# Attention with routed experts: VectorE copies the accumulator out unscaled, GpSimdE joins the halves and multiplies by reciprocal sums turned to 64 partitions

## What is computed

```python
q, k, v = x @ Wq + bq, x @ Wk + bk, x @ Wv + bv      # 8 heads ("d") of width h = 64
scores = jnp.einsum('bdsh,bdth->bdst', q, k) / np.sqrt(8)
weights = jax.nn.softmax(scores, axis=-1)
feats = jnp.einsum('bdst,bdth->bdsh', weights, v)    # S = 2048 rows, 2048 keys
x = layernorm(x + feats.reshape(B, S, F) @ Wo + bo)
# then, per row: top 6 of 64 experts by sigmoid(x @ w_gate), capacity 256 rows per expert,
# silu(g) * v of x @ w_up[e], times w_down[e], weighted sum; plus a shared expert
x = layernorm(x + shared + routed)
```

## Time and profile before

| | us |
|---|---|
| median of 3 runs | 1292.33 |
| lowest, highest | 1290.95, 1292.90 |
| span of the profiled execution | 1289.5 |
| TensorE busy in the span | 1255.7 (97%) |
| VectorE, ScalarE, GpSimdE busy | 998.2, 919.8, 513.2 |

### The profile page before, as it was taken

The page is one execution under the profiler, slowest core; times in us unless marked ns, Lnnn a source line. Parts: engine busy times, 40 slices in busy tenths (PEclk is TensorE's granted clock), DMA queues, the critical chain, the costliest instruction groups (busy, mean ns, idle before and its releaser), DMA issues. The chain is left out here.

```text
span 1289.5 us, 24161 instructions
## 1 busy us (share of the span) xinstructions
PE 1255.7 (97%) x8128; PEld 1058.8 (82%) x8128; DVE 998.2 (77%) x1891; ACT 919.8 (71%) x1643; POOL 513.2 (40%) x508
## 2 busy tenths in 40 slices
PE   7999999999999999999999999999988999999896
PEld 5888799889889889989989989989866877777642
DVE  5623688789889979979979979979866777776387
ACT  5421589778878868868868868878833877778343
POOL 0002223234524524524533533542543666676412
PEclk9999999999999999999999999999999999999999
DMA  8788466212424424323423423543578999997698
GB/s 282 258 283 289 155 196 223 69 42 84 147 66 138 145 70 139 125 88 110 146 84 101 155 89 88 156 136 120 178 272 326 386 386 385 346 339 252 237 426 335
DMA packets 90951, 253.14 MB, mean 196 GB/s; under 512 B 16824, under 2 KB 39480, under 8 KB 87504
## 3 DMA queue, kind: packets, MB, share of 16 engines
q1 hardware_dynamic: 70608, 196.78, 44.9%
q0 software_dynamic: 17920, 50.62, 10.2%
q10 hardware_dynamic: 2304, 4.20, 0.8%
HBM read 177.87 MB, written 134.91 MB: 243 GB/s over the span
## 5 line engine op out<-in xcount | busy, mean ns | idle before, releaser
L967 ACT ACTIVATE p_hi<-slot 128x512 fp32r<-128x512 f32 x512 | 278.5, 596 | 108.9 <-PE slot L1594 105.5
L807 POOL TENSOR_TENSOR p_lo<-prob,p_hi 128x512 fp32r<-128x512 f32 x128 | 166.1, 1297 | 441.9 <-ACT prob L969 441.7
L1607 PE MATMUL slot<-k_stack,q_stack 128*128 128x512 f32 x1024 | 300.1, 415 | 0.0
L984 ACT ACTIVATE prob<-prob,row_min 128x1024 f32<-128x1024 f32 x256 | 296.8, 1160 | 0.1
L1307 DVE TENSOR_TENSOR p_lo<-slot,p_hi 128x512 fp32r<-128x512 f32 x384 | 250.8, 681 | 52.5 <-ACT p_hi L967 51.1
L1594 PE MATMUL slot<-ident,prob 128*128 128x128 f32 x2048 | 265.8, 273 | 1.3 <-ACT prob L984 1.3
L1632 PE MATMUL pv_acc<-p_hi,v_pair 128*128 128x256 f32 x1024 | 263.1, 290 | 2.6 <-POOL p_lo L807 1.8
L1632 PE MATMUL pv_acc<-p_lo,v_pair 128*128 128x256 f32 x1024 | 253.7, 281 | 0.0
L1594 PEld LDWEIGHTS slot<-ident,prob 128*128 128x128 f32 x2048 | 229.5, 141 | 1.9 <-issue 1.7
L1632 PEld LDWEIGHTS pv_acc<-p_hi,v_pair 128*128 128x128 f32 x1024 | 192.6, 188 | 16.1 <-issue 5.7
L1632 PEld LDWEIGHTS pv_acc<-p_lo,v_pair 128*128 128x128 f32 x1024 | 192.8, 188 | 12.9 <-issue 3.3
(11 more groups left out here) (196 smaller groups left out, 1974.4 us busy)
## 6 DMA issues: line engine op xcount, KB each, us to landing
disp_hbm<-zero_hbm SPq DMA_DIRECT2D x64, 518.0 KB, 6.3
rows_all<-disp_hbm SPq DMA_DIRECT2D x64, 518.0 KB, 12.8
y_hbm<-zero_hbm SPq DMA_DIRECT2D x48, 512.0 KB, 4.4
got<-y_hbm SPq DMA_DIRECT2D x15, 1536.0 KB, 19.0
q_stack<-q_hbm SPq DMA_DIRECT2D x128, 128.0 KB, 3.1
up_pair<-in_L_ffn_w_up SPq DMA_DIRECT2D x26, 512.0 KB, 9.5
down_w<-in_L_ffn_w_down SPq DMA_DIRECT2D x32, 256.0 KB, 12.0
q_hbm<-q_hi SPq DMA_DIRECT2D x8, 512.0 KB, 2.7
```

The source lines that it names most:

```text
L807: e.tensor_tensor(p_lo[1][:, 2:4, :], prob[:, m % 2, :, (4 * u + 2) * P:(4 * u + 4) * P], p_hi[1][:, 2:4, :].bitcast(F32), ALU.subtract).t ...
L967: e.activation(p_hi[b][:, two, :], view[:, two, :], ACT.Copy).then_inc(a_phi, 1)
L984: e.activation(keys, keys, ACT.Exp, bias=row_min[:, me % 2, j, 1:2], scale=-1.0, accum_out=row_sum[:, me % 2, j, half:half + 1]).then_inc( ...
L1607: made = e.matmul(slot[:, n * BANK:(n + 1) * BANK], qs[:, part, j * P:(j + 1) * P], k_stack[:, ms % H, keys], start=part == 0, stop=part == 1)
```

## The change

VectorE copies `pv_acc` to `acc` without scaling; it no longer waits for ScalarE's copy nor for the transfer to `feats`, but for the join of the head before. TensorE turns `row_inv` to 64 partitions only, and ScalarE's copy goes to its own buffers `inv_all`. GpSimdE joins in place in `moved`, one step later than before, and multiplies by `inv_all`. The transfer to `feats` goes out two steps later. `moved` and `feats` are doubled and `resid` has four buffers; the scratch of the queue for indirect transfers is set to 4096 bytes per partition. The parts of a chunk's end move by three ticks, on all engines. The zeroing transfers of `disp_hbm` and `y_hbm` are spread otherwise.

```diff
@@ buffers
-        scaled = sb("scaled", [P, QC], F32, att)
-        moved = sb("moved", [P, QC], F32, att)
-        feats = sb("feats", [P, H // 2, QC], F32, att)
+        acc = sb("acc", [P, QC], F32, att)
+        moved = [sb("moved0", [P, QC], F32, att)]
+        feats = [sb("feats0", [P, H // 2, QC], F32, att)]
...
+        moved.append(sb("moved1", [P, QC], F32, att))
+        feats.append(sb("feats1", [P, H // 2, QC], F32, att))
+        inv_all = [sb(f"inv_all{i}", [P, QC], F32, att) for i in range(2)]
+        resid += [sb(f"resid{i}", [P, WITH], F32, att) for i in range(QT, 2 * QT)]
@@ ticks and head_out
-        P0, P1 = 14, 38
+        P0, P1 = 17, 41
...
             if m % 2:
                 e.wait_ge(d_feats, 16 * (m // 2 + 1))
             else:
-                e.wait_ge(g_join, m + 1)
+                e.wait_ge(g_scaled, m + 1)
@@ SyncE
-                elif c:
-                    e.wait_ge(d_scat[j], 16 * TOPK * c)
-                    e.wait_ge(d_st, 16 * 2 * c)
+                elif c >= 2:
+                    e.wait_ge(d_scat[j], 16 * TOPK * (c - 1))
+                    e.wait_ge(d_st, 16 * 2 * (c - 1))
...
-            for s in range(LAST + LAG + 2):
+            for s in range(LAST + LAG + 4):
+                mj, uj = divmod(s - LAG - 2, STEPS)
+                if mj >= 0 and uj == STEPS - 1:
+                    e.wait_ge(v_acc_out, mj + 1)
+                    if mj >= 2:
+                        head_out(e, mj - 2)
+                    e.dma_start(moved[mj % 2][0:D, :], acc[D:P, :]).then_inc(d_moved, 16)
+                mf, uf = divmod(s - LAG - 4, STEPS)
+                if mf >= 0 and uf == STEPS - 1 and mf % 2:
+                    e.wait_ge(g_scaled, mf + 1)
+                    e.dma_start(feats_of(mf // H)[D:P, (mf % H) // 2, :], moved[1][0:D, :]).then_inc(d_feats, 16)
...
-                if mv >= 0 and uv == STEPS - 1:
-                    e.wait_ge(v_scaled, mv + 1)
-                    e.dma_start(moved[0:D, :], scaled[D:P, :]).then_inc(d_moved, 16)
-                    if mv % H == H - 1 and mv // H < END:
-                        jobs.append(chunk_end(mv // H))
-                mj, uj = divmod(s - LAG - 2, STEPS)
-                if mj >= 0 and uj == STEPS - 1 and mj % 2:
-                    e.wait_ge(g_join, mj + 1)
-                    e.dma_start(feats[D:P, (mj % H) // 2, :], moved[0:D, :]).then_inc(d_feats, 16)
+                if mv >= 0 and uv == STEPS - 1 and mv % H == H - 1 and mv // H < END:
+                    jobs.append(chunk_end(mv // H))
...
-                elif 2 * STEPS <= s < 2 * STEPS + E - Z_EARLY:
-                    zero_disp(range(Z_EARLY + s - 2 * STEPS, Z_EARLY + s - 2 * STEPS + 1))
-                elif s % 4 == 0 and E <= s < E + 4 * NZ:
-                    e.dma_start(y_pieces[(s - E) // 4], zero_hbm[:, 0:2 * C]).then_inc(d_yzero, 16)
+                elif s >= 2 * STEPS and s % STEPS < 2:
+                    first = Z_EARLY + 3 * (s // STEPS - 2) + 2 * (s % STEPS)
+                    zero_disp(range(first, min(first + 2 - s % STEPS, E)))
+                if s % STEPS == 1 and E <= s < E + STEPS * NZ:
+                    e.dma_start(y_pieces[(s - E) // STEPS], zero_hbm[:, 0:2 * C]).then_inc(d_yzero, 16)
@@ GpSimdE
-                yield from to(10)
+                yield from to(13)
                 root(c, 0)
...
-                mj, uj = divmod(s - LAG - 2, STEPS)
+                mj, uj = divmod(s - LAG - 3, STEPS)
                 if mj >= 0 and uj == STEPS - 1:
-                    e.wait_ge(v_scaled, mj + 1)
+                    joined = moved[mj % 2][0:D, :]
+                    e.wait_ge(v_acc_out, mj + 1)
                     e.wait_ge(d_moved, 16 * (mj + 1))
-                    e.wait_ge(p_proj, 2 * (mj // H))
-                    target = moved[0:D, :] if mj % 2 else feats[0:D, (mj % H) // 2, :]
-                    e.tensor_tensor(target, scaled[0:D, :], moved[0:D, :], ALU.add).then_inc(g_join, 1)
+                    e.tensor_tensor(joined, acc[0:D, :], joined, ALU.add).then_inc(g_join, 1)
+                    c, k = mj // H, (mj % H) // 2
+                    if c >= 2:
+                        e.wait_ge(p_proj, 2 * (c - 1))
+                    e.wait_ge(g_join, mj + 1)
+                    e.wait_ge(a_spread, mj + 1)
+                    e.tensor_tensor(
+                        joined if mj % 2 else feats_of(c)[0:D, k, :], joined, inv_all[mj % 2][0:D, :],
+                        ALU.mult).then_inc(g_scaled, 1)
@@ ScalarE
                     e.wait_ge(p_spread, m + 1)
-                    if m:
-                        head_out(e, m - 1)
-                    e.activation(scaled[:, :], misc[:, 0:QC], ACT.Copy).then_inc(a_spread, 1)
+                    if m >= 2:
+                        e.wait_ge(g_scaled, m - 1)
+                    e.activation(inv_all[m % 2][0:D, :], misc[0:D, 0:QC], ACT.Copy).then_inc(a_spread, 1)
@@ VectorE (its chunk_end: 6, 8, 10, 12 become 9, 11, 13, 15)
-                    e.wait_ge(a_spread, mv + 1)
-                    e.wait_ge(p_pv, 4 * mv + 4)
+                    e.wait_ge(p_pv, STEPS * (mv + 1))
                     if mv:
-                        head_out(e, mv - 1)
-                    e.tensor_tensor(scaled[:, :], pv_acc[:, 0:QC], scaled[:, :], ALU.mult).then_inc(v_scaled, 1)
+                        e.wait_ge(g_join, mv)
+                    e.tensor_copy(acc[:, :], pv_acc[:, 0:QC]).then_inc(v_acc_out, 1)
@@ TensorE
-                yield from to(5)
+                yield from to(8)
                 out_project(c, 0)
-                yield from to(9)
+                yield from to(12)
                 out_project(c, 1)
...
                     if uv == 0 and mv:
-                        e.wait_ge(v_scaled, mv)
+                        e.wait_ge(v_acc_out, mv)
...
-                        made = e.transpose(misc[:, j * P:(j + 1) * P], row_inv[:, j:j + 1].to_broadcast([P, P]),
+                        made = e.transpose(misc[0:D, j * P:(j + 1) * P], row_inv[:, j:j + 1].to_broadcast([P, D]),
                                            ident[:, :])
@@ program
-    nc = _bacc.Bacc("TRN2", target_bir_lowering=False, num_devices=1)
+    nc = _bacc.Bacc("TRN2", target_bir_lowering=False, num_devices=1, dynamic_dma_scratch_size=4096)
```

35 lines of the change are left out of this document (20 added, 15 removed).

## The result

| | before | after |
|---|---|---|
| median of the runs, us | 1292.62 (1290.95 to 1293.61, 4 runs) | 1298.65 (1297.66 to 1301.69, 4 runs) |
| profiled execution: its time, its span, us | 1290.95, 1289.5 | 1298.82, 1297.1 |
| first product of `pv_acc`, last product of the attention, us | 154.55, 939.07 | 154.40, 946.84 |
| output projection of chunks 0 and 6 starts at, us | 249.86, 849.07 | 253.62, 860.53 |
| mean chunk between these (a sixth), us | 99.87 | 101.15 |

A forecast was written before the change was run, and what follows sets the result against it. TensorE was taken to bound the attention, busy 784.2 of 789.0 us. A stall of +3.9 us and a gain of 0.7 made +3.2 on the 1292.3 us median: 1295.5 us, range 1290.5 to 1300.

The forecast's parts named there:

- the likeliest case: Outcome slower than before, given 0.47, against 0.40 for the same and 0.13 for faster.
- The stall behind four scatters and the bias: At ends of chunks 1 to 6, GpSimdE's queue makes `p_lo` late for TensorE by 0.65 us: +3.9 us.
- the small stall of the earlier trace: In before, `p_lo` of the step before a chunk's head 7 ends came 0.14 us late; expected to go.
- The turning at e+3: Turning of the sums, three steps after head 7 of a chunk ends, no longer waits for `misc`: -0.7 us.
- "Cost on the path: 0" for VectorE: VectorE's 64 products become same-size copies and lose two waits: cost 0, gain at most 0.5 us.
- "`p_lo` behind tile 0's scatters, covered by 0.4": At tile 0's scatters `p_lo` starts 1.1 us late, still in time for TensorE: 0, up to 2 us in the range.
- The narrow load 0: TensorE's `row_inv` transposes with 64 instead of 128 stationary columns: load doesn't set their pace, gain 0.
- Product on GpSimdE hidden: One more 64x256 operation per head, 64 x 0.8 = 51 us, hidden on GpSimdE wherever its queue isn't full.
- Transfer of `feats`, tail, scratch, expert phase: 0: Later `feats` transfer covered by 0.3 us, tail by 0.4; smaller scratch taken as 0; expert phase unchanged.
- The 2.8 us that the sum puts outside the span: Median of before, 1292.3 us, less its profiled span, 1289.5 us, taken to lie outside the span.
- Rival 3: GpSimdE fails at more places: slower product and join or `feats` landing use up three thin covers, +6, 1301 us; chance 0.12.

The follow-up runs named there:

- e5_bias_late: after, with GpSimdE's bias addition for tile 0 of a chunk three steps later: 1297.09 us, ratio to before 1.0039.
- e4_wide_turn: after, with TensorE turning `row_inv` to 128 partitions again instead of 64: 1300.55 us, ratio to before 1.0057.
- e12_tail_wide: e9 with TensorE turning `row_inv` to 128 partitions again instead of 64: 1290.64 us, ratio to before 0.9981.
- e2_no_product: after, without GpSimdE's multiplication, so the join writes its target directly and features stay unscaled: 1298.25 us, ratio to before 1.0036.
- e11_small_scratch: before, with only the scratch for GpSimdE's indirect DMAs set to 4096: 1291.55 us, ratio to before 0.9990.
- e9: e7 with the last chunk's bias additions two steps later and head 62's join and product behind the last `p_lo`: 1289.14 us, ratio to before 0.9975.
- e7: after, with two scatters per four side steps and the score addition also giving a row result: 1292.8 us, ratio to before 1.0001.
- e3_score_accum: after, with VectorE's score addition in a form that also writes an accumulator nothing reads: 1294.76 us, ratio to before 1.0011.
- e8: before, with only the chunk-end ticks three later, `feats` and `resid` doubled and the smaller scratch; VectorE still scales: 1307.75 us, ratio 1.0122.
- e6_scatter_spread: after, with GpSimdE issuing two scatters for every four side steps instead of every two: 1293.37 us, ratio to before 1.0000.

## Where the prediction was right and where it was wrong

The forecast was 1295.5 us in a range of 1290.5 to 1300; the time is 1298.65, in the range and slower, as the likeliest case had it, but 3.2 us above it. The direction rests on a stall that was forecast rightly. That the time lies in the range is in good part luck: the largest term of the loss was priced at nothing, and the range was wide enough for another reason. Point by point:

- **The stall behind four scatters and the bias: right in place, count and cause, a little too large.** Forecast 0.65 us, six times, called net of the small stall of the earlier trace rows though 0.14 wasn't taken off; measured 0.66, and less that 0.14 it is 0.52: +3.1 us instead of +3.9. The order of GpSimdE's queue came out instruction by instruction as laid out, with `p_lo` to `p_lo` 7.54 us against 7.63 worked out. e5_bias_late shows the cause.
- **The turning at e+3 no longer waits for `misc`: right.** It starts 0.12 behind the last product (351.69 and 351.81) where the earlier trace rows had 0.21: -0.1, seven times.
- **"Cost on the path: 0" for VectorE: this is the step that failed.** I priced VectorE's edited operation (rightly: the copy takes 424 ns as the product did, and its waits brought nothing) and asked of every shifted tick whether a *semaphore* would come late. VectorE's other operations have no semaphore against GpSimdE, so they were in no list. But the addition of the scores moved to a place beside join, product and `p_lo`, stood there for 1.83 us instead of 0.19, and pushed the cast behind it beside the next `p_lo`. That is 6 x 0.85 = +5.1 us, the largest term of the whole sum.
- **"`p_lo` behind tile 0's scatters, covered by 0.4": right, and beside the point.** TensorE never waited for that `p_lo`; the same late `p_lo` cost 0.85 us through VectorE. I had worked out its lateness (1.1 us), and asked only one engine about it.
- **The narrow load 0: right**, in this kernel (e4_wide_turn) and where no stall could hide a gain (e12_tail_wide); the pace of the gate had pointed there. The Trainium skill (TensorE: Matmul & The Clock Gate, section LDWEIGHTS (loading the stationary operand)) has the load's time go by the columns of the stationary operand, so half for half of them; the trace shows less than that, 107 ns against 134.
- **Product on GpSimdE hidden: right only for its own queue.** In the body of the attention it delayed no `p_lo` that TensorE waited for. But it was a part of what held VectorE's addition: without it that stall is gone and another of nearly its size comes, 0.2 us a chunk on balance (e2_no_product). **Transfer of `feats`, tail, scratch, expert phase: 0, right.** The projection starts at 354.77, where its cover was thin, with no wait; the scratch was tried by itself (e11_small_scratch). The 2.8 us that the sum puts outside the span are a difference between a median and one span; the profiled execution itself took 1290.95 us, 1.5 more than its span. The forecast adds its terms to the median, so nothing hangs on it.
- **Rival 3, failure at more places, was the case that came closest** in time (1301) and came for another reason than the ones it listed. Its chance of 0.12 was for covers running out, not for a cost without a semaphore.

The sum with the measured terms: 3.1 + 5.1 - 0.7 = +7.5 us, against 7.9 in the attention of the two traces and 6.0 in the medians.

The failed term could have been read from the trace of before. Two lines of VectorE there, at the end of the same chunk:

```profile
345.93 0.75 DVE L1343 TENSOR_TENSOR row_inv<-row_sum 128x2 f32<-128x2 f32 x1
...
346.80 0.57 DVE L1243 SCALAR_TENSOR_TENSOR weight_of<-small,top 128x6 f32<-128x6 f32 x1
```

Operations on 2 and 6 columns, for 0.75 and 0.57 us. The first ends at 346.68 and the `p_lo` of the earlier trace rows at 346.66; the second at 347.37 and the join at 347.33. Before was paying this price already, off the path.

## What to carry to other kernels

When side work is moved to other steps, ask of every small operation of VectorE what GpSimdE does on SBUF at that moment, as well as who waits for whom: a blocked operation carries no wait, only a length far over the shortest of its group, and it ends when GpSimdE's does. Look for such lengths in the profile before costing a shift at nothing. And where a change's gain is eaten by where its side work falls, the place can be mended by itself: here spreading the scatters to two per `p_lo` and letting no transfer stand in front of the last one turned +6.0 us into -3.2 (e9 also has the other form of the addition, which gave nothing more in e7). When an edit leaves the list of waits nearly as it was, compare the times at which the waits stand: the same sum can be another stall.

## What the runs showed of the hardware that was not expected

- **An addition on 128x64 takes 0.19 us alone and 1.83 us beside GpSimdE's operations on SBUF; in its form with a row result it takes 0.22 us beside them** (e3_score_accum). Held operations of VectorE ended 0.03 to 0.06 us after GpSimdE's at the places read (318.75 and 318.69 in after, 348.41 and 348.38 there; 353.13 and 353.10, 390.11 and 390.07 in e8; 354.24 and 354.20 in e2).
- **Back-to-back operations of GpSimdE can hold one operation of VectorE through more than one of them:** the addition at 316.92 outlasted product and `p_lo`, and the 2.00 us at 351.13 in e8 join and `p_lo`. It isn't so every time: at 345.93 in before (above) VectorE got in at the end of `p_lo`, with the join right behind. What decides isn't shown.
- **It works both ways.** Of a pair that starts within 0.01 us either can be the one held (VectorE 1.15 us instead of 0.56 in e12, GpSimdE 1.17 instead of 0.74 in e9), and the last `p_lo` of e9, 0.4 us into a subtraction of VectorE on 128x1024, takes 1.92 us instead of 1.28.
- **A stationary operand of half the columns loads in 107 instead of 134 ns,** and nothing of it reaches the end: the interval around the pair of transposes is 0.33 us with either.
- **The clock granted to TensorE late in the kernel varies between executions.** The stretch from 960 to 1100 us in before and in e6_scatter_spread, whose expert phases are the same code:

```profile
960.00:1100.00 140.00, 133.61 (x938) 105.37 (x938) 102.41 (x180) 94.16 (x143) 82.88 (x76) 1.00 0.97 373
```

```profile
960.00:1100.00 140.00, 133.58 (x925) 105.99 (x926) 99.85 (x175) 92.55 (x140) 79.94 (x74) 0.98 0.97 367
```

  Two hundredths of 140 us are, as an estimate, up to 2.8 us, about the size of the effects looked for. From the first transpose behind the attention to the end it is 350.1 us in after (mean granted clock of the execution 0.999) and 354.4 in e12_tail_wide (0.995). That is why chunk periods decide here and medians only confirm.
- **The clock fell behind an idle stretch of 3.06 us** in e6 and e7 (0.50 from 938 to 940 us), where it had been 1.00; behind idle stretches of 1.54 us in before, 1.53 in e9 and 1.97 in after at the same place it stayed at 1.00.
